# Mixing products of a fused four-layer attention kernel, two mixings at a time

## What is computed

```python
xa = _ln(x, ln1_w, ln1_b)
sx = previous_token(xa) - xa
xxx = jnp.tanh((xa + sx * maa_x) @ maa_w1).reshape(b, l, 5, 32)
xxx = jnp.einsum('blfd,fde->blfe', xxx, maa_w2)
xm = xa[:, :, None] + sx[:, :, None] * (maa_stack + xxx)
xk, xw, xv, xr, xg = (xm[:, :, j] for j in range(5))
w = jnp.exp(-jnp.exp(time_decay + jnp.tanh(xw @ td_w1) @ td_w2))
r, k, v, g = xr @ Wr.T, xk @ Wk.T, xv @ Wv.T, silu(xg @ Wg.T)
```

## Time and profile before

| | |
|---|---|
| device time, median of 3 runs | 1957.99 us (1957.55 to 1958.88) |
| profiled execution, first to last instruction | 1957.6 us |
| PE busy | 1663.1 us (85%), 13615 matmul instructions |
| DVE busy | 1235.2 us (63%) |
| ACT busy | 939.7 us (48%) |
| POOL busy | 812.5 us (42%) |
| mean granted TensorE clock | 0.931 |

### The profile page before, as it was taken

The page is one execution under the profiler, slowest core; times in us unless marked ns, Lnnn a source line. Parts: engine busy times, 40 slices in busy tenths (PEclk is TensorE's granted clock), DMA queues, the critical chain, the costliest instruction groups (busy, mean ns, idle before and its releaser), DMA issues.

```text
span 1957.6 us, 36688 instructions
## 1 busy us (share of the span) xinstructions
PE 1663.1 (85%) x13615; PEld 1032.1 (53%) x13615; DVE 1235.2 (63%) x2121; ACT 939.7 (48%) x1855; POOL 812.5 (42%) x903
## 2 busy tenths in 40 slices
PE   5888898889997898898987989978998889888735
PEld 3565555565563655555554645646455465556203
DVE  3743478645786468844786457854688546973483
ACT  4454554545554445545544455544555544453202
POOL 4531248404573147702485034830467113760070
PEclk8998999998999899998998989989999989999857
DMA  6001014200331005100141102310052000410070
GB/s 179 2 2 35 1 20 53 45 18 1 44 41 33 18 1 67 24 27 18 18 55 34 29 1 36 49 34 18 1 61 30 27 18 9 59 24 13 1 87 11
DMA packets 73583, 60.92 MB, mean 31 GB/s; under 512 B 38960, under 2 KB 56512, under 8 KB 73408
## 3 DMA queue, kind: packets, MB, share of 16 engines
q1 hardware_dynamic: 55648, 47.99, 17.2%
q10 hardware_dynamic: 17216, 10.55, 1.9%
q0 software_dynamic: 544, 0.03, 0.0%
HBM read 20.28 MB, written 4.19 MB: 13 GB/s over the span
## 4 chain that ended last, share of the span: by engine, by line
PE 54%; DVE 18%; ACT 10%; issue 9%; POOL 6%; DMA 1%; DVEq 0%; ACTq 0%; POOLq 0%; SPq 0%
PE bank L627 21%; PE bank L766 7%; PE bank L1008 6%; PE bank L643 4%; PE bank L899 3%; PE bank L946 2%; DVE seg_max L1472 2%; POOL soft_ring L1684 2%; ACT soft_ring L1145 2%; PE bank L971 2%; PE bank L886 2%; DVE late L1322 1%; DVE late L1310 1%; PE bank L706 1%; PE bank L781 1%
## 5 line engine op out<-in xcount | busy, mean ns | idle before, releaser
L1684 POOL TENSOR_TENSOR soft_ring<-soft_ring,seg_max 128x512 f32<-128x512 f32 x256 | 286.8, 1135 | 308.5 <-DVE seg_max L1472 307.8
L1164 ACT ACTIVATE soft_ring<-soft_ring 128x512 f32<-128x512 f32 x256 | 160.5, 627 | 195.0 <-POOL soft_ring L1684 180.9
L1310 DVE TENSOR_TENSOR_SCAN late<-late 128x520 f32<-128x520 f32 x128 | 222.4, 1738 | 35.2 <-POOL late L1640 16.5
L1638 POOL TENSOR_TENSOR late<-late 128x520 f32<-128x520 f32 x128 | 192.3, 1502 | 90.5 <-DMA late<-late 58.3
L766 PE MATMUL bank<-early 32*128 32x128 f32 (+2 forms) x1024 | 155.2, 422 | 50.7 <-ACTq L1148 46.4
L946 PE MATMUL bank<-ident,soft_ring 128*128 128x128 f32 x1024 | 164.4, 290 | 17.5 <-ACT soft_ring L1164 13.0
L1472 DVE TENSOR_REDUCE seg_max<-soft_ring 128x8 f32<-128x512 f32 (+1 forms) x256 | 167.0, 676 | 6.8 <-DVE early L1522 2.1
L946 PEld LDWEIGHTS bank<-ident,soft_ring 128*128 128x128 f32 x1024 | 116.0, 145 | 93.7 <-issue 57.4
L1692 POOL TENSOR_SCALAR soft_ring<-soft_ring,rden 128x256 f32<-128x256 f32 x64 | 61.8, 966 | 239.4 <-DVE rden L1430 239.4
L1036 ACT ACTIVATE late<-bank 128x512 f32<-128x512 f32 (+2 forms) x104 | 62.0, 596 | 166.2 <-PE bank L627 162.9
L627 PE MATMUL bank<-early,w 128*128 128x512 f32 x256 | 119.8, 619 | 18.4 <-ACT early L1226 18.4
(11 more groups left out here) (255 smaller groups left out, 3348.5 us busy)
## 6 DMA issues: line engine op xcount, KB each, us to landing
late<-late SPq DMA_DIRECT2D x128, 260.0 KB, 4.4
c<-in_ctx ACTq DMA_DIRECT2D x8, 512.0 KB, 4.0
x<-in_x ACTq DMA_DIRECT2D x8, 512.0 KB, 4.9
out_x<-late SPq DMA_DIRECT2D x8, 512.0 KB, 2.9
mask<-in_mask_Bx1xSxS_ff ACTq DMA_DIRECT2D x16, 128.0 KB, 3.9
mask<-in_mask_BxS_ik SPq DMA_DIRECT2D x8, 256.0 KB, 3.2
w<-in_L_xattn_mlp_w SPq DMA_DIRECT2D x2, 1024.0 KB, 9.8
wkv<-in_L_xattn_kv_w SPq DMA_DIRECT2D x1, 512.0 KB, 3.8
```

The source lines that it names most:

```text
L1164: af(soft[:, u % SOFT, :], soft[:, u % SOFT, :], ACT.Exp).then_inc(sig("exp"), 1)
L1310: nc.vector.tensor_tensor_scan(sj[:, n % 2, :], wP[:, k, :, :].rearrange("p b t -> p (b t)"), aj[:, n % 2, :], 0.0, ALU.mult, ALU.add).the ...
L1638: tt(aj[:, n % 2, :], kP[:, k, :, :].rearrange("p b t -> p (b t)"), vj[:, n % 3, :], ALU.mult).then_inc(sig("kv_done"), 1)
L1684: tt(s, s, seg_max[:, u % SOFT, 0:segs].unsqueeze(2).broadcast_to([128, segs, 512 // segs]), ALU.subtract).then_inc(sig("sub"), 1)
```

## The change

The mixings are taken in pairs, (1, 0) and (2, 3), and mixing 4 alone. A stage is now one half of the channels for both mixings of a pair: mix 0 and mix 1 are the halves of the first pair, mix 2 and mix 3 those of the second, and mix 4 has both halves of the fifth mixing. For each part PE first takes a late bank for each mixing and then issues the products, each with the 32 rows that hold its weights instead of 128. The stage mix 3 moves ahead of decay: its slot on PE from 42 to 36, on DVE from 42 to 36. DVE reads the parts in the new order, and the counts of `xm_ready` for which td, k, v, r and g wait become 3, 4, 7, 8 and 10 (before 2, 4, 6, 8 and 10).

```diff
-        STAGES = (["moments", "normalize", "turn", "shift", "maa", "mix 0", "mix 1", "td", "k", "mix 2", "decay", "v",
-                   "mix 3", "mix 4", "r", "g", "r u k", "bonus"] + [("scan", n) for n in range(SCANS)] +
+        STAGES = (["moments", "normalize", "turn", "shift", "maa", "mix 0", "mix 1", "td", "k", "mix 2", "mix 3", "decay", "v",
+                   "mix 4", "r", "g", "r u k", "bonus"] + [("scan", n) for n in range(SCANS)] +
                   ["center", "variance", "gate", "project", "moments 2", "normalize 2", "turn 2", "shift 2", "ffn k", "ffn r", "ffn v"])
         MIXES = (1, 0, 2, 3, 4)
+        MIX_PARTS = (((0, 0),), ((0, 1),), ((2, 0),), ((2, 1),), ((4, 0), (4, 1)))
+        MIXED = (3, 4, 7, 8, 10)
...
-            "mix 3": (42, 40, 42, 35),
+            "mix 3": (36, 33, 36, 35),
...
-                    def mix(f):
-                        for m in range(KT):
-                            product((stage, m), 512, [(maa2[:, f, 128 * m:128 * m + 128], xf[:, f // 4, :])], "late")
+                    def mix(n):
+
+                        for first, m in MIX_PARTS[n]:
+                            held = [(f, fill(pe, "late", (f"mix {first + i}", m))) for i, f in enumerate(MIXES[first:first + 2])]
+                            for f, (t, full) in held:
+                                r = 32 * (f % 4)
+                                mm(t[:, :], maa2[r:r + 32, f, 128 * m:128 * m + 128], xf[r:r + 32, f // 4, :],
+                                   start=True, stop=True).then_inc(full, 1)
...
-                        pe.wait_ge(sig("xm_ready"), past("xm_ready") + KT * (n + 1))
+                        pe.wait_ge(sig("xm_ready"), past("xm_ready") + MIXED[n])
...
-                        mix(MIXES[int(stage[4])])
+                        mix(int(stage[4]))
...
-                        pe.wait_ge(sig("xm_ready"), past("xm_ready") + KT)
+                        pe.wait_ge(sig("xm_ready"), past("xm_ready") + MIXED[0])
...
-                    def mix(n, f):
-
-                        if n:
-                            filled({1: "maaB", 2: "td", 3: ("k", 1), 4: ("v", 1)}[n])
-                        for k in range(KT):
-                            t, free = take(dve, (stage, k))
-                            m = xm[:, (n + 1) % 2, k, :]
-                            link(stt(out=m, in0=t[:, :], scalar=v("maa", 2 * f + k), in1=sx[:, k, :], op0=ALU.add, op1=ALU.mult))
-                            dve.sem_inc(free, 1)
-                            tt(batches(m), batches(m), xaP[:, k, :, 1:LP], ALU.add).then_inc(sig("xm_ready"), 1)
+                    def mix(part):
+
+                        for first, k in MIX_PARTS[part]:
+                            for n, f in enumerate(MIXES[first:first + 2], first):
+                                if k == 0 and n:
+                                    filled({1: "maaB", 2: "td", 3: ("k", 1), 4: ("v", 1)}[n])
+                                t, free = take(dve, (f"mix {n}", k))
+                                m = xm[:, (n + 1) % 2, k, :]
+                                link(stt(out=m, in0=t[:, :], scalar=v("maa", 2 * f + k), in1=sx[:, k, :], op0=ALU.add, op1=ALU.mult))
+                                dve.sem_inc(free, 1)
+                                tt(batches(m), batches(m), xaP[:, k, :, 1:LP], ALU.add).then_inc(sig("xm_ready"), 1)
...
-                        n = int(stage[4])
-                        mix(n, MIXES[n])
+                        mix(int(stage[4]))
```

## The result

The changed kernel takes 2030.60 us (median of 4 runs, 2030.20 to 2031.08) against 1958.29 us for the kernel before: a ratio of 1.036, 95% interval 1.0344 to 1.0377. It is 72 us slower. The forecast was slower by 38 us, with a range that ended at 2010 us, so the direction was right and the size was half of what came.

What follows compares the result with a forecast made beforehand. PE bounds k to r; per overlapped block -0.5 (ahead of k) + 6.4 (waits) - 2.3 (given back after v) = +3.6 us, seven blocks +25, last block +2.3, giving 1985.6 us; clock +10 gives 1996 us, range 1980 to 2010.

Steps and rivals of the forecast that it cites:

- What bounds the kernel: From k to r in seven overlapped blocks: PE is busy 22.78 of 22.97 us, so its work or waiting counts fully.
- The pairing's price and the waits: Per overlapped block: a pair takes 1.06 us instead of 1.71; PE idles about 2.0 us, then 2.8 us.
- pair 3: Stage mix 2, behind k: waits until ACT empties both banks, ends at 481.53; nothing gained, 0.1 us lost.
- pair 4: Stage mix 3 at PE slot 36, ahead of the scores: waits for DVE's second reading, PE idle about 2.0 us.
- the trip through scores, masking and maximum: Ahead of decay: DVE reads the mixing only after these, PE idles another 2.8 us; PE 6.4 us later there.
- the upper end that the forecast gave it: Mix 4's lone 32-row products: 0.2 us a product for changing tiles, 0.4 us a block; the forecast kept 0.
- Pairs 1 and 2: Stages mix 0 and mix 1, ahead of k: 0.5 us gained per block, the rest lost waiting for DVE.
- The clock: Behind the new PE idles: one fall in six of seven blocks at 1.7 us, +10 us; bounds none and +24 us.
- The last block: No softmax between stages: +1 us at k, +4.4 us k to v, -3.1 us v to r; +2.3 us, bounds 0 and 5.5.
- the clock stays up: Rival: same waits, but no fall of the clock in nearly all blocks, 1986 us; chance 0.21.
- the round trips are hidden: Rival: PE's waits at slots 36 and 37 come under 2.8 us per block, kernel faster, down to 1937 us; chance 0.04.
- the pairs do not overlap: Rival: three pairs on the path each cost 0.65 us more per block, 14 us in all, 2010 us; chance 0.07.

Runs made afterwards that it cites:

- e2: Changed kernel with VectorE's reading of the second pair's second half one slot earlier (35 instead of 36), ahead of masking and maximum: 1995.70 us, ratio 1.0179.
- e3: Changed kernel with only the second half of the second pair moved behind decay (PE and DVE slot 39): 1968.01 us, ratio 1.0037 to the kernel before.
- e1: Changed kernel with unused products filling PE's waits, two ahead of the second pair's second half, three ahead of decay: 1995.65 us, ratio 1.0178.
- e4: Changed kernel with 128-row instead of 32-row mixing products, so the two of a pair run one after the other: 2020.93 us, ratio 1.0302.
- e5: Kernel before with the first pair alone (mix 0 and mix 1 in halves side by side), other mixings in old places: 1966.06 us, ratio 1.0028.
- e6: Changed kernel with the old order and single 128-row products in the last block alone: 2022.21 us, ratio 1.0317.
- e11: Kernel before with three unused products at each of three other places per overlapped block where PE idles about 3 us: 1960.08 us, ratio 0.9999.
- e13: Changed kernel with the second pair's second half behind decay and the last block as in the kernel before: 1960.27 us, ratio 0.9994.

## Why the prediction was wrong in its size

**What bounds the kernel** was right: PE filled the stretch, and what PE lost there reached the end.

**The pairing's price and the waits** were right in kind, and nearly in size. A pair takes 1.06 us; pair 3 waits for ACT and gains nothing; pair 4 waits for DVE's second reading; decay waits for the trip through scores, masking and maximum. e2 showed that trip by taking it away, e3 by moving the half out of it. At full clock (e1) the stretch is 27.74 us, where the forecast's terms give 22.97 + 6.4 - 2.3 = 27.1 us. Of the missing 0.6 us, 0.2 us is mix 4: from v to the next scores it takes 5.88 us with two 32-row products (505.88 to 511.76) and 5.68 us with two of 128 rows (e4), 0.1 us a product. The Trainium skill, TensorEngine Tiling (Array Packing), section Key Properties, says that a change of the tiling mode drains TensorE; these 0.2 us fit that, at half of the upper end that the forecast gave it, but no run separates a drain from other costs of a lone 32-row product. Another 0.2 us is decay's second half, which takes 1.05 us by itself (493.04 to 494.09 in e1) where the forecast had 0.86. With the gain ahead of k taken off, the waits of the seven blocks cost some 32 us, 7 us more than the forecast's 25.

**Pairs 1 and 2** gained 0.2 to 0.4 us (e5) instead of 0.5 us.

**The clock** is the step that failed: "I take one fall of the clock in six of the seven blocks, at 5.40 - 3.70 = 1.7 us: +10 us. Bounds: none, and two per block (+24 us)." Measured: the seven stretches from k to r are together 160.8 us long before, 218.7 us after, and 194.9 us in e1, where the clock stays at 1.00 in them. So the waits cost 34 us there and the clock 24 us, about 3.4 us a block; over the whole kernel, filling both waits gives 35 us (1.036 - 1.0178 = 0.0182).

What was wrong is which work the fall meets. It begins already in the shorter wait, ahead of pair 4, in all seven blocks, and with the next wait following the clock stays down for 10 to 14 us. In the block shown pair 4, the scores, decay and most of the query product run in that time, which adds 4.0 us, where the forecast had one short fall behind decay at 1.7 us. That its upper bound, two such falls per block, is 24 us too is a coincidence: it is one long fall.

The forecast took its price from eight products behind a single idle time. A nearer case stood in the trace of the kernel before, ahead of the mixing in the same block: two idle times, here for ACT in the softmax of layer 0, with 3.7 us of work between them, and a clock that is down for some 10 us. PE's timeline, and the table by windows below it:

```profile
440.61 1.13 PE L766 MATMUL bank<-early 64*128 64x256 f32 x8 [3.32 <-ACTq L1148]
...
446.15 2.08 PE L766 MATMUL bank<-early 64*128 64x256 f32 x8 [1.80 <-ACTq L1148]
...
442.50:452.50 10.00, 8.20 (x34) 5.42 (x33) 4.96 (x11) 7.59 (x20) 3.13 (x3) 0.52 0.01 2
```

The scores behind the first idle time take 1.13 us there, those behind the second 2.08 us, and in six of the seven blocks those behind the second take 2.08 us.

**The last block** was mis-sized as well: +2.3 us forecast, 8.4 us measured (e6). The places were right (pair 2 waits 2.48 us, td 1.65 us, pair 4 2.54 us), but the clock was left out there; k to r ran at a granted clock of 0.80 (1.00 before), and v came 15.4 us behind k where the forecast had 12.4.

Together, by the two profiled executions (2028.6 against 1957.6 us): of 71 us, 58 us lie in the seven stretches (34 us of waits and 24 us of clock), 7 us in the last block from maa to r, and the remaining 6 us in the rest of the program, most of them between r and the maa of the next block. In e1 that part is no longer than before, so of e1's 35 us some 10 us came from outside the stretches. Which falls of the clock cost them there is not shown.

**The rivals.** That the clock stays up is refuted by the 0.50 in all seven blocks. That the round trips are hidden is refuted by the two waits. That the pairs do not overlap is refuted by the 1.06 us, and e4 showed that this rival's sign was wrong in the changed order: with no overlap the kernel is faster, not 14 us slower.

## What to carry to other kernels

Before work is made shorter by running it side by side, look at what stands behind it: a pair that takes all banks of a ring at once starts with the last reader and leaves nothing for PE to do meanwhile. Where a stage is moved ahead of another on the same ring, follow the reader's own queue: here one slot on DVE (36 instead of 35) stood behind work that waited for PE. And a new idle time on a busy PE can cost more than its own length: price at half clock all the work behind it, up to where a trace of the same kernel shows the clock coming back after waits like these, and look for the place in the trace whose waits are most like the new ones.

## What the runs showed of the hardware that was not expected

- In an idle time of 1.96 us, with 0.82 us of idle time a little ahead of it, the granted clock went from 1.00 to 0.50 in all seven blocks; with 1.28 us in its place (e4) it stayed up until the next wait of 2.77 us.
- Between the pieces of work that ran at half speed the waits kept their length (2.77 us against 2.75 us in e1): the slow work was paid for once.
- PE work whose results nobody uses made the kernel 35 us faster (e1), and products with four times the rows, three quarters of them zeros, made it about 10 us faster (e4).
- Holding the clock up at three other idle places raised its mean from 0.931 to 0.942 and did not change the time (e11). Why the gain did not come through was not settled; the falls moved to other places of the block.
- A spared 0.45 us per block, on an engine that was busy all the while, could not be found in the total (e13): the executions of one kernel differ by up to 9 us.
